# A convolution, attention and top-1 expert kernel: the split of four experts moved, the norm and the gate moved to other engines

## The reference

```python
x = x + conv(groupnorm(x))       # 1x1 conv on channels and 28 correlations with nearby pixels
t = tokens(x)                    # 8 images of 256 rows of 192
t = t + attn(layernorm(t))       # causal softmax attention in one head, within an image
gate = layernorm(t) @ Wg.T + bg  # 8 experts; each row goes to the best one
t = t + W3[e] @ (silu(W1[e] @ n) * (W2[e] @ n))   # n: layernorm(t) of the row; W1, W2: 469 x 192
```

## Time and profile before

| | us |
|---|---|
| median of 3 runs | 240.7 (239.81 to 241.13) |
| the profiled execution | 241.94 |
| its span in the trace | 240.1 |
| TensorE busy | 212.7 |
| VectorE busy | 173.5 |
| ScalarE busy | 115.4 |
| GpSimd busy | 97.6 |
| mean granted TensorE clock | 0.936 of 2.4 GHz |

### The profile page before, as it was taken

The page is one execution under the profiler, slowest core; times in us unless marked ns, Lnnn a source line. Parts: engine busy times, 40 slices in busy tenths (PEclk is TensorE's granted clock), DMA queues, the critical chain, the costliest instruction groups (busy, mean ns, idle before and its releaser), DMA issues.

```text
span 240.1 us, 4737 instructions
## 1 busy us (share of the span) xinstructions
PE 212.7 (89%) x1340; PEld 189.9 (79%) x1340; DVE 173.5 (72%) x580; ACT 115.4 (48%) x235; POOL 97.6 (41%) x112
## 2 busy tenths in 40 slices
PE   6987999989799798988897679999999999999970
PEld 3676898978698688878785468999999999999960
DVE  4596998564778889887867828788777767686741
ACT  2285764432988797777640013433434343434410
POOL 3245423520199699989546000313132222313131
PEclk9998999999999999997755959999999999999997
DMA  6991344449006644653711122332210000010000
GB/s 230 371 312 46 87 127 143 155 104 409 19 0 227 229 131 148 244 196 93 267 35 50 50 67 54 94 87 55 79 36 1 33 8 22 19 34 2 33 12 0
DMA packets 15767, 25.87 MB, mean 108 GB/s; under 512 B 3799, under 2 KB 12691, under 8 KB 14720
## 3 DMA queue, kind: packets, MB, share of 16 engines
q1 hardware_dynamic: 13872, 22.40, 28.4%
q0 software_dynamic: 1872, 3.18, 3.8%
HBM read 19.50 MB, written 6.76 MB: 109 GB/s over the span
## 4 chain that ended last, share of the span: by engine, by line
PE 60%; DVE 20%; ACT 8%; issue 6%; POOL 2%; DMA 2%; POOLq 1%; SPq 0%; DVEq 0%; ACTq 0%
PE bank L1326 7%; PE bank L1302 4%; PE bank L1034 4%; PE bank L1038 4%; PE bank L1037 4%; PE bank L1036 4%; PE bank L1035 4%; PE bank L1327 3%; DVE wall L797 3%; PE bank L1218 3%; PE bank L1317 2%; PE bank L1076 2%; PE bank L1045 2%; PE bank L1184 1%; PE bank L1029 1%
## 5 line engine op out<-in xcount | busy, mean ns | idle before, releaser
L462 POOL DMA_INDIRECT out_rows<-yo,rows x23 | 22.3, 972 | 81.8 <-DVE yo L1007 78.6
L1326 PE MATMUL bank<-wall,HH 128*128 x92 | 29.4, 374 | 1.5 <-DVE HL L987 1.5
L992 DVE TENSOR_TENSOR gh<-gh,bank 128x470 f32<-128x470 f32 x23 | 14.8, 646 | 20.5 <-PE bank L1038 20.5
L627 ACT ACTIVATE HH<-bank 128x512 fp32r<-128x512 f32 x23 | 13.8, 600 | 27.9 <-PE bank L1302 27.9
L1327 PE MATMUL bank<-wall,HL 128*128 x92 | 23.1, 252 | 0.0
L633 ACT ACTIVATE FH<-bank 128x256 fp32r<-128x256 f32 x23 | 8.9, 385 | 28.4 <-PE bank L1317 28.4
L1034 PE MATMUL bank<-wall,FH 128*128 x46 | 19.7, 429 | 1.1 <-DVE FL L995 1.1
L416 POOL DMA_INDIRECT token_rows<-rows,posi x16 | 16.7, 1044 | 6.8 <-issue 4.5
L630 ACT ACTIVATE gh<-bank 128x470 f32<-128x470 f32 x23 | 13.0, 565 | 13.4 <-PE bank L1038 13.4
L1326 PEld LDWEIGHTS bank<-wall,HH 128*128 128x128 f32 x92 | 17.3, 188 | 1.8 <-issue 1.7
L987 DVE TENSOR_TENSOR HL<-bank,HH 128x512 fp32r<-128x512 f32 x23 | 15.9, 691 | 3.5 <-ACT HH L627 3.4
(11 more groups left out here) (233 smaller groups left out, 680.8 us busy)
## 6 DMA issues: line engine op xcount, KB each, us to landing
stage<-in_w_all SPq DMA_DIRECT2D x8, 1324.0 KB, 6.0
rows<-token_rows SPq DMA_DIRECT2D x23, 98.0 KB, 2.0
near_rows<-gram SPq DMA_DIRECT2D x8, 243.0 KB, 3.0
xcm<-in_x_cm SPq DMA_DIRECT2D x2, 768.0 KB, 8.3
rows<-in_x_tm SPq DMA_DIRECT2D x1, 1536.0 KB, 13.8
token_rows<-emptyt SPq DMA_DIRECT2D x3, 294.0 KB, 3.7
taps_sb<-near_rows SPq DMA_DIRECT2D x8, 103.0 KB, 2.1
small_sb<-in_small SPq DMA_DIRECT2D x1, 704.0 KB, 8.1
```

The costliest lines, as they stand in the source:

```text
L462: pool.indirect_dma_start(out=out, out_offset=bass.IndirectOffsetOnAxis(ap=rows[:, j, C + 2:C + 3].bitcast(U32), axis=0), in_=yo[:, par], ...
L992: nc.vector.tensor_tensor(gh[:, par, 0:FE], gh[:, par, 0:FE], bank[2 + 2 * par][:, 0:FE], ALU.mult).then_inc(gh_ready, 1)
L1326: nc.tensor.matmul(dst[:, 0:2 * C], HH[:, 1 - par, k], w(0, P, c0, c0 + 2 * C), start=(k == 0), stop=False)
```

## The change

1. **Experts.** GpSimd splits experts 0 to 3 in attention, VectorE their leftovers. Between table and first slot VectorE splits expert 4 (four pieces and the leftover) and takes expert 5's leftover; GpSimd then takes expert 5's low parts. Expert 6's raw values are loaded early into the place of its own low parts in `wall` (its third piece late, over the attention's scratch); ScalarE copies its high parts in the last step, GpSimd takes its low parts behind the first two sends and VectorE its leftover behind slot 3. Expert 7 is loaded into `stage[0]` once expert 4 is split; ScalarE copies its high parts behind its norms in slots 2, 3 and 4, VectorE takes the low parts behind slots 4 and 5 and the leftover behind slot 6. TensorE's waits stay as they are.
2. **The norm of the slots' rows** goes from VectorE to ScalarE, which needs -mean/std as a bias; VectorE writes it (`shift_of`). ScalarE's loop over the slots is written out.
3. **The gate.** The rows get eight more columns. The values' weights get 2 x 8 more (`VW = C + 16`): the row itself times the gate, and v times the gate. So the P·V product brings the attention's part of the logits along, and adding it to the row adds it to the logits. The row's own part is copied from PSUM with a scale by ScalarE, twice a step. Turning the finished rows, copying them and multiplying them by the gate is gone, and with it step 10; the gates and positions of images 6 and 7 are both in step 9. In steps 3 to 7 the gate comes ahead of the leftover and the positions behind it.
4. The two subtractions of U's low parts are one.

The core of the diff:

```diff
-SPLIT_LAST = EXPERTS - 2
+SPLIT_LAST = EXPERTS - 4
+IN_PLACE = EXPERTS - 2
...
+            sp.dma_start(raw_wall[:, W12:2 * W12], w_all[IN_PLACE][:, 0:W12]).then_inc(place_in, 16)
+            sp.dma_start(raw_w3, w_all[IN_PLACE][:, 2 * W12:STAGE].rearrange("p (k c) -> p k c", c=C)).then_inc(place_in, 16)
+            for e in range(2, IN_PLACE):
                 sp.wait_ge(wall_lo, e - 1)
                 sp.wait_ge(wall_q, e - 1)
                 weights_in(e)
+            sp.wait_ge(o_ready, IMAGES + AHEAD)
+            sp.dma_start(raw_b, w_all[IN_PLACE][:, W12:2 * W12]).then_inc(raw_b_in, 16)
...
+            for j in range(4):
+                load_slot(j, j % 2, j // 2 if j > 1 else None)
+            sp.wait_ge(wall_lo, EXPERTS - 3)
+            sp.wait_ge(wall_q, EXPERTS - 3)
+            sp.dma_start(stage[:, 0], w_all[EXPERTS - 1]).then_inc(stage_in[0], 16)
...
+                nc.scalar.activation(V[:, par], v[:, :, EXPERTS:VW], ACT.Copy)
+                for h in range(HALVES):
+                    j = 2 * t + h
+                    ins = nc.scalar.activation(rows_all[:, j, 0:EXPERTS], v[:, h, 0:EXPERTS], ACT.Copy, scale=ln1s[:, j:j + 1])
+                ins.then_inc(v_copied, 1)
...
+            def norm_slot(j, par, loaded):
+                sc.wait_ge(slot_in[par], 16 * loaded)
+                sc.wait_ge(nb_ready, j + 1)
+                sc.wait_ge(fxt_ready, j + AHEAD)
+                row = rows[:, j]
+                nb, rs = row[:, C:C + 1], row[:, C + 1:C + 2]
+                nc.scalar.activation(xf[:, 0:C], row[:, 0:C], ACT.Identity, scale=rs, bias=nb)
+                nc.scalar.activation(xf[:, C:2 * CA], row[:, CA:C], ACT.Identity, scale=rs, bias=nb).then_inc(fx_ready, 1)
...
+                if 2 <= j < 5:
+                    weights_hi((0, 1, 2)[j - 2], EXPERTS - 1)      # ScalarE, behind ffn_step(j)
...
+                if i == LAG + 3:                                    # VectorE; TensorE makes v times the gate
+                    ve.wait_ge(vg_sum, 1)
+                    link(nc.vector.tensor_copy(vg[:, :, EXPERTS:2 * EXPERTS], bank[0][:, 0:2 * EXPERTS].rearrange("p (t e) -> p t e", t=2)))
...
-            low_weights(EXPERTS - 2, range(6))
+            low_weights(SPLIT_LAST, range(4))
+            leftover(SPLIT_LAST)
+            shift_of(0, 0, 1)
+            leftover(SPLIT_LAST + 1)
...
-                if 0 <= j < 6:
-                    low_weights(EXPERTS - 1, (j,))
+                if j == 3:
+                    leftover(IN_PLACE, 2)
+                if j in (4, 5):
+                    low_weights(EXPERTS - 1, (2 * j - 8, 2 * j - 7))
+                if j == 6:
+                    leftover(EXPERTS - 1, 2)
```

More of the change, by code:

```diff
@@ L99 @@
 _at = 0
-for _n, _w in (("gm", 4 * CA), ("cf", 2 * C), ("taps", C), ("place", TAPS), ("beside", P), ("wq", 4 * CA), ("wk", 4 * CA), ("wv", 2 * C)):
+for _n, _w in (("gm", 4 * CA), ("cf", 2 * C), ("taps", C), ("place", TAPS), ("beside", P), ("wq", 4 * CA), ("wk", 4 * CA), ("wv", 2 * C), ("wvt", 4 * CA)):
     S1[_n] = (_at, _at + _w)
@@ L194, in build @@
         ln1v = sb("ln1v", [P, TILES], ctx=middle)
+        ln1s = sb("ln1s", [P, TILES], ctx=middle)
         lnv = sb("lnv", [P, HALVES], ctx=middle)
@@ L616, in _ @@
             sc.wait_ge(empty_out, 16 * HEAD_PARTS)
-            for t in range(1, IMAGES + 3):
+            for t in range(1, IMAGES + 2):
                 step(t, t % 2)
@@ L842, in step @@
                     for h in range(HALVES):
-                        row = rows[:, bass.ds(2 * t + (h - 4), 1), 0:C].rearrange("p a c -> p (a c)")
-                        ins = nc.vector.scalar_tensor_tensor(out=row, in0=bank[5][:, C * h:C * (h + 1)], scalar=rsum[:, h:h + 1], in1=row,
+                        row = rows_all[:, 2 * t + (h - 4), 0:VG]
+                        ins = nc.vector.scalar_tensor_tensor(out=row, in0=bank[5][:, VG * h:VG * (h + 1)], scalar=rsum[:, h:h + 1], in1=row,
                                                              op0=ALU.mult, op1=ALU.add)
                     ins.then_inc(o_taken, 1)
-                if on(t, 3) and t >= IMAGES:
-                    gate(t, link)
+                if t == IMAGES:
+                    gate(t - 3, link)
                 if on(t, 2):
@@ L935, in _ @@
             ve.wait_ge(empty_out, 16 * HEAD_PARTS)
-            for t in range(2, IMAGES + 3):
+            for t in range(2, IMAGES + 2):
                 step(t, t % 2)
@@ L1145, in turn_image, with counts @@
                 mm.then_inc(xt_ready, 1)
-            def turn_rows(t):
-                pe.wait_ge(o_taken, t - 1 + AHEAD)
-                pe.wait_ge(x2_copied, t - 2 + AHEAD)
-                for part in range(2):
-                    for h in range(HALVES):
-                        at = PIX * part + P * h
-                        mm = nc.tensor.transpose(bank[6][:, at:at + P], rows[:, 2 * t + (h - 4), CB * part:CB * part + P], ident)
-                mm.then_inc(t2t_ready, 1)
-            def counts(t):
-                pe.wait_ge(oh_ready, t - 2 + AHEAD)
+            def counts(b):
+                pe.wait_ge(oh_ready, b + 1 + AHEAD)
                 before, all_ = tri_sb[:, 0:P], tri_sb[:, P:2 * P]
@@ L1198, in step @@
                 if t == IMAGES:
-                    counts(t)
+                    counts(t - 3)
                 if on(t, 1):
```

310 lines of the change are left out of this document (163 added, 147 removed).

## The result

The changed kernel is slower: 245.68 us at the median of 4 runs (244.9 to 247.15) against 240.6 us, ratio 1.022 with a 95% interval of 1.017 to 1.027. The prediction (241.5, range 238.8 to 244.2) missed it by 4.2 us. The traces of e_gate, h_ctl and k_refit are of executions 0.5 to 1.4% above their medians; lengths of steps, waits, landings and half-clock stretches are read from them, no totals.

What follows compares the result with a forecast made beforehand. No single engine bounds it: TensorE in the slots, ScalarE (steps 1, 2) and VectorE (3 to 7) in attention. 0.65 + 0.2 - 4.3 + 0.5 + 3.75 = +0.8 us: 241.5 beside the median of 240.7, range 238.8 to 244.2.

Steps and rivals of the forecast that it cites:

- the clock's fall behind the stall: Rival, slots 7 to 9: TensorE's clock falls in slot 7's stall, losing 1.65 to 3.3 us; chance 0.26.
- the small delays: Slot steps 3 to 6: ScalarE's expert 7 copies and VectorE's splits make products late, +1.5 us in sum.
- worth nothing by themselves: Attention steps: they don't wait for TensorE, so its 1.5 us of removed matmuls a step gain nothing.
- Convolution, +0.85: Convolution stage: four small matmuls and six VectorE instructions, +0.65 us, and one more GpSimd product per token factor, +0.2.
- Attention, -4.3: Attention steps and tail: the longer of VectorE's and ScalarE's loops, step by step, -4.3 us; bounds -5.4 and -3.0.
- the small copies: ScalarE in attention: two scaled 8-column copies a step, 0.29 us each, 0.6 a step; bounds 0.15 and 0.44 each.
- The rival's last sentence: Attention, end of the clock rival: a second clock fall in the lighter steps costs 1 to 1.9 us likewise.
- Handover, +0.5 for the norm: Attention to first slot: VectorE's shift, a hop and two ScalarE instructions take 1.15 us for 0.65, +0.5.
- stall of step 7, +2.25: Slot 7: TensorE waits for expert 7's leftover, queued on VectorE behind slot 5's output; 2.25 us, nothing hides it.
- hidden, 0.4 us to spare: Slots: with the norm on ScalarE, HH starts 0.2 us late, but HL still ends 0.4 us before it delays TensorE.
- by the rows it is 0.6, hidden: Slots 2 or 3: a VectorE instruction meeting a GpSimd one costs 0.6 us, hidden, so the sum stands.
- The prediction's 2.2 us for one meeting: Slots 2 or 3: by the skill's exclusion rule one VectorE-GpSimd meeting costs up to 2.2 us, making the sum 243.7.

Runs made afterwards that it cites:

- e_gate: Kernel before with the gate columns alone; experts split as before, slots' norm on VectorE, no attention fillers: ratio 0.997 to the kernel before.
- h_ctl: Kernel before with twelve 8-column filler matmuls ahead of its 26 long ones, as a control: ratio 1.000.
- k_refit: Changed kernel with attention fillers, one-input shift, expert 7's copies and the leftovers of experts 6 and 7 earlier: ratio 0.989 to the kernel before.
- f_attfill: Changed kernel with ten 256-column filler matmuls on TensorE in each attention step from 2 to 7: ratio 1.013 to the kernel before.
- l_normact: i_gatefill with the slots' norm on ScalarE and the one-input shift on VectorE, experts split as before: ratio 0.993 to the kernel before.
- i_gatefill: e_gate with ten 256-column filler matmuls in each attention step from 2 to 7: ratio 0.982 to the kernel before.
- g_ts: Changed kernel with VectorE's one-column shift as tensor_scalar with one tensor input instead of two: ratio 1.018 to the kernel before.
- n_hit: j_warm with four 512-column and twenty-one 8-column fillers per attention step instead of ten of 256: 251.54 us, ratio 1.039 to the kernel before.
- j_warm: i_gatefill with 36 long fillers behind the last counts instead of 26: 237.59 us, ratio 0.980 to the kernel before.
- d_normv: Changed kernel with the norm of the slots' rows back on VectorE (two instructions, no shift): ratio 1.022 to the kernel before.

## Why the prediction was wrong

It forecast +0.8 us and the profiled run had +5.3 of span. The 4.5 between them are, but for 0.1, the last scatter's landing (+2.1, a term that the sum put at nothing), the clock's fall behind the stall (+1.6, a rival left out of the sum), the small delays (+0.8), the first slot's start (+0.3) and attention (-0.4). In the runs the step that failed most plainly is the one on TensorE's lighter load in attention, "worth nothing by themselves": over six traces attention took 1.7 us longer on average than in f_attfill, where TensorE has fillers. Term by term:

- **Convolution, +0.85.** Right: second XH +0.89.
- **Attention, -4.3.** Right in the profiled run, -4.7, though in part because errors cancel: steps 1 to 3 took 7.5 to 7.7 us for 7.9, 7.9 and 8.2, step 5 8.6 for 7.9. The steps that it read off the kernel before also add up to 71.4 us, where the stretch is 71.9 long; with that put right the same terms give -4.8. VectorE's last part (reciprocal to last positions) took 7.43 us for 7.5; steps 7 and 8 took 7.3 and 5.7 for 6.6 and 5.3; the small copies start 0.15 us apart, so a pair costs ScalarE's loop 0.3, the lower bound and not the 0.6 taken. But this stood for one execution with one half-clock stretch; in the six traces without attention fillers the gain is 2.7 to 4.7, with them in f_attfill 5.3. The step that failed is the sentence "TensorE is not what these steps wait for, so its 1.5 us are worth nothing by themselves". Taken out, they left TensorE busy 39 to 41 of 50 us for 43.1, and all six traces without attention fillers of kernels with both gate columns and the rearranged experts have one to three half-clock stretches there, each costing a step about 1 us; e_gate has three. The kernel before had one in its trace (at 107.0) and none in two others; with the work put back as filler there is at most one. The runs agree: 0.997 without and 0.982 with fillers, intervals apart. The rival's last sentence priced a single one at 1 to 1.9 us.
- **Handover, +0.5 for the norm.** Right: slot 0's transposes begin 1.18 us after the shift (135.00 to 136.18) where they began 0.65 after the norm, +0.5 here and in l_normact. The other 0.3 of the measured +0.8 lie behind: the transposes took 0.70 us for 0.44, since the half-clock stretch began at 135.5, ahead of them, and at 137.8 before. What no step held is the last scatter's landing, +2.1 us in the profiled run: I moved instructions of TensorE and never asked where its own instructions come in.
- **Slots, stall of step 7, +2.25.** Right: 2.12 us idle, +2.3.
- **Slots, small delays, +1.5.** Mis-sized: +2.3. Steps 3 to 5 measured +0.99, +0.47 and +0.55 for the list's 0.4, 0.3 and 0.7, and step 1 +0.31, for which there was no term. Step 1 is the norm's move to ScalarE, 4.07 us in i_gatefill and 4.78 in l_normact, which the prediction had "hidden, 0.4 us to spare" in every slot; from step 2 on it is. (Less shows against the kernel before, whose step 1, 4.36, began at half clock.) Step 3 is the meeting with GpSimd. The prediction took GpSimd's split beside VectorE as "0" and "by the rows it is 0.6, hidden". GpSimd held VectorE's one-column shift until its own end, three times (0.93, 0.67, 0.50 us for 0.15), and in step 3 the shift stands ahead of ScalarE's norm, copy and HH: 0.46 us, by g_ts. The Trainium skill (SBUF — State Buffer, Who interferes with whom) says that such a pair excludes each other for the whole instruction, and the trace agrees: the shift ended at 152.22, GpSimd at 152.19. The prediction's 2.2 us for one meeting was its upper end; the three added 0.8, 0.5 and 0.3 to the shift, because the two overlap only in part. The error was to take a wait as hidden off rows of attention in which VectorE had time to spare.
- **The rival that came true in the profiled run.** The clock at half behind the stall, +1.65 to 3.3 and a chance of 0.26: +1.6. With the landing and 0.8 of small delays beside it the forecast for the profiled execution, 242.7, becomes 247.2, and 247.15 was measured. The runs' medians don't divide so well: the fall came in three of five traces, and moving the packet alone changed nothing that they show.

By parts, with TensorE filled in attention: gate columns with these fillers -1.8% (i_gatefill), without them -0.3%, inside the spread (e_gate); ScalarE's norm +1.0% (l_normact), of which its trace accounts for half; the experts' new order no difference that can be told (k_refit to l_normact, -0.3%) if its pieces are queued in time, and +2% as written (f_attfill to l_normact, the two-input shift with it).

Open: what the late landing costs in the runs (seen in traces only, and two attempts to put it back missed), whether the stall causes the fall behind it, and what the attention fillers would give the kernel before.

## What to carry to other kernels

Work taken from the engine with the throttled clock isn't free even if nobody waits for that engine: look at its busy share after the cut, and put a filler where it stands. A piece that is moved behind a wait of its engine's queue must be followed to its last consumer, and two instructions that are each hidden, on GpSimd and VectorE, need not be when one of them stands ahead of a third engine's norm. Where a long-tuned handover grows by 2 us with nothing changed in it, look at the instruction packets on the DMA engines before blaming the transfer.

## What the runs showed of the hardware that was not expected

- Instructions come in 16 KB packets, 0.9 to 1.7 us each on one DMA engine. That these are TensorE's is argued: they lie some 250 of its recorded instructions apart, and fillers on TensorE moved one from 130.04 to 125.72 us. The Trainium skill (Runtime: NRT & Kernel Launch, Instruction fetch mechanics) gives the same 16 KB blocks and calls their cost mostly hidden. For TensorE the trace agrees (from 130.0 to 131.2 us it is busy 1.20 of 1.20 us); for a scatter it doesn't: in the five traces with a packet close behind the issue its last share landed 1.3 to 2.0 us behind the other fifteen.
- TensorE's clock fell while the profile shows the engine busy without a gap: in n_hit, 3.4 us at 0.50 and 6.8 at 1.00 in turn, where bursts of 8-column matmuls stood among wide ones. With ten fillers of 256 columns in their place (j_warm) it stayed at 1.00 from 57 to 107 us.
- A VectorE instruction with one SBUF tensor of 192 columns (tensor_scalar in d_normv) waits for GpSimd as well: 2.18 us where the others take 0.37. The same form on one column (g_ts) doesn't: 0.20 us throughout.
